# Projection stage of a decoder kernel: who copies the transposed tiles, and in which order VectorE and ScalarE take their steps

## What is computed

```
q = x Wq^T (32 heads of 128)   k = x Wk^T (8 heads)   v = x Wv^T (8 heads)
q, k = rmsnorm(q) * q_norm_w, rmsnorm(k) * k_norm_w      per head
q, k = rope(q), rope(k):  [t1 cos - t2 sin, t2 cos + t1 sin]
attention over 512 cached keys in pages and 32 new ones, then Wo
```

## Time and profile before

| what | value |
|---|---|
| median of three runs | 2634.18 us (2633.91 to 2634.66) |
| the profiled execution | 2633.39 us, its span 2631.6 us |
| busy over the span | PE 2530.8 us, VectorE 1653.0, ScalarE 1236.4, GpSimd 742.3 |
| projection stage | from the start to about 688 us |
| blocks of q and k | to about 608 us |

### The profile page before, as it was taken

One profiled execution on the slowest core, in us unless ns is written; L12 is line 12 of the kernel. 1 busy time (PEld: TensorE's weight loads), 2 busy tenths in 40 slices (PEclk: granted clock), 3 DMA queues, 4 the chain that ended last, 5 costly groups with the idle time before them and its releaser, 6 DMA issues. The chain is left out here.

```text
span 2631.6 us, 48525 instructions
## 1 busy us (share of the span) xinstructions
PE 2530.8 (96%) x15312; PEld 2178.8 (83%) x15312; DVE 1653.0 (63%) x3906; ACT 1236.4 (47%) x3285; POOL 742.3 (28%) x783
## 2 busy tenths in 40 slices
PE   5899999999999999999999999999998799999998
PEld 4677777778799999999999999999997577777776
DVE  8999999992366666666666666666666433333332
ACT  5555555552355555555555555555555222222221
POOL 5877777773021111211112111122111200000000
PEclk9999999999999999999999999999999899999999
DMA  3233233236598888888888888888885222322221
GB/s 139 81 97 94 82 112 90 86 96 211 164 340 272 265 267 265 270 274 267 265 263 270 272 272 265 266 267 266 283 258 192 80 90 90 96 84 88 88 87 44
DMA packets 369851, 484.13 MB, mean 184 GB/s; under 512 B 50320, under 2 KB 304528, under 8 KB 366480
## 3 DMA queue, kind: packets, MB, share of 16 engines
q1 hardware_dynamic: 332816, 347.67, 42.6%
q0 software_dynamic: 36864, 134.23, 14.3%
HBM read 393.70 MB, written 88.08 MB: 183 GB/s over the span
## 5 line engine op out<-in xcount | busy, mean ns | idle before, releaser
L821 ACT ACTIVATE probs<-probs,neg_max 128x544 f32<-128x544 f32 x512 | 383.5, 749 | 559.2 <-DVE neg_max L870 559.2
L893 PE MATMUL s_bank<-k_t,q_t 128*128 128x288 f32 (+1 forms) x2048 | 556.5, 394 | 4.6 <-POOL v_own L784 3.6
L910 PEld LDWEIGHTS o_bank<-p_t,v_c 128*128 128x128 f32 x4096 | 537.5, 192 | 26.3
L910 PE MATMUL o_bank<-p_t,v_c 128*128 128x128 f32 x4096 | 539.7, 275 | 0.0
L839 DVE COPY p_t<-pt_a 128x256 f32<-128x256 f32 x512 | 217.9, 426 | 417.4 <-PE pt_b L921 417.4
L893 PEld LDWEIGHTS s_bank<-k_t,q_t 128*128 128x128 f32 x2048 | 350.2, 191 | 60.0 <-POOL v_own L784 4.1
L441 POOL TENSOR_TENSOR q_t<-normed,v_c 128x256 f32<-128x256 f32 x320 | 337.8, 1076 | 147.8 <-ACT normed L490 147.8
L870 DVE CUSTOM_DVE_ANT_0 probs<-s_bank,mask 128x544 f32<-128x544 f32 x512 | 367.1, 717 | 3.9 <-PE s_bank L893 3.9
L656 PE MATMUL acc<-w_hi,x_hi 128*128 128x512 f32 x768 | 318.0, 414 | 14.7 <-DVE x_lo L541 14.7
L657 PE MATMUL acc<-w_lo,x_hi 128*128 128x512 f32 x768 | 304.4, 396 | 0.0
L658 PE MATMUL acc<-w_hi,x_lo 128*128 128x512 f32 x768 | 303.1, 395 | 0.0
(11 more groups left out here) (128 smaller groups left out, 3739.4 us busy)
## 6 DMA issues: line engine op xcount, KB each, us to landing
k_t<-in_k_pages SPq DMA_DIRECT2D x1024, 128.0 KB
q_spill<-wo_early SPq DMA_DIRECT2D x32, 1024.0 KB, 5.1
q_t<-q_spill SPq DMA_DIRECT2D x64, 512.0 KB
o_spill<-o_t SPq DMA_DIRECT2D x64, 512.0 KB, 8.8
raw<-o_spill SPq DMA_DIRECT2D x64, 512.0 KB, 3.5
k_t<-in_w_qkv SPq DMA_DIRECT2D x12, 1024.0 KB, 7.9
k_spill<-wo_early SPq DMA_DIRECT2D x8, 1024.0 KB, 5.1
v_spill<-wo_early SPq DMA_DIRECT2D x8, 1024.0 KB, 4.8
```

Source lines behind the costliest of these rows:

```text
L821: nc.scalar.activation(probs[:, j % 4], probs[:, j % 4], ACT.Exp, scale=-1.0, bias=neg_max[:, j % 2:j % 2 + 1], accum_out=row_sum[:, j % 2 ...
L893: last = pe.matmul(s_bank[:, columns].rearrange("p (s t) -> p s t", t=PSIZE), q_t[:, par, g], k_t[:, par, slots, g], start=True, stop=True)
L910: last = pe.matmul(o_bank, values, p_t[:, i, c], start=c == 0, stop=c == KC)
```

## The change

Three things change in the list of each engine for a q or k block:

- the copy of the transposed block n-4 moves from VectorE to ScalarE, ahead of the root;
- ScalarE drains block n-1 and then squares block n; before it was the other way round;
- VectorE multiplies block n-2 first, then takes the reciprocal of block n-1, adds block n-2, and sums block n's squares last.

TensorE, GpSimd and the queue of SyncE keep their lists.

```diff
 ScalarE, for each block
+                        if lag in ("q", "k"):
+                            m, t = n - 4, (j - 4) % NT
+                            act.wait_ge(flipped, m + 1)
+                            ...
+                            nc.scalar.activation(to.rearrange("p (b h s) -> p b h s", h=HS, s=S),
+                                                 flip[j % 2][:, :].rearrange("p (h b s) -> p b h s", h=HS, s=S),
+                                                 ACT.Copy).then_inc(staged_qk, 1)
...
                             nc.scalar.activation(rms[:, i], sumsq[:, i], ACT.Sqrt, bias=eps[:, 0:1], scale=1.0 / HD)
-                        if kind != "v":
-                            act.wait_ge(mm_done, n + 1)
-                            nc.scalar.activation(squares ... ACT.Square).then_inc(squared, 1)
                         if lag in ("q", "k"):
                             act.wait_ge(rstd_done, n)
...
                             last.then_inc(drained, 1)
+                        if kind != "v":
+                            act.wait_ge(mm_done, n + 1)
+                            nc.scalar.activation(squares ... ACT.Square).then_inc(squared, 1)
 VectorE, for each block
+                        rope = kind if j >= 2 else before
+                        m, i, t = n - 2, j % 2, (j - 2) % NT
+                        if rope in ("q", "k"):
+                            at_least(dve, roped_done, m)
+                            dve.wait_ge(drained, m + 1)
+                            nc.vector.tensor_tensor(part_s, normed[:, i], straight[rope] ..., ALU.mult)
                         if (kind if j >= 1 else before) in ("q", "k"):
                             dve.wait_ge(rooted, n)
+                            nc.vector.reciprocal(rstd[:, 1 - i], rms[:, 1 - i]).then_inc(rstd_done, 1)
+                        if rope in ("q", "k"):
+                            dve.wait_ge(straight_done, m + 1)
+                            dve.wait_ge(crossed_done, m + 1)
+                            at_least(dve, flipped, m - 1)
+                            nc.vector.tensor_tensor(roped[:, i], part_s, part_c[:, i], ALU.add)
-                        (the copy of flip to stage, with its waits on flipped and stored)
                         if kind != "v":
                             dve.wait_ge(squared, n + 1)
                             nc.vector.tensor_reduce(sumsq[:, j % 2], squares[:, j % 2], AX.X, ALU.add)
-                        (the product and the addition of block n-2, which stood here)
```

More of the change, by code:

```diff
@@ L476, in emit @@
                         n = p * PS + j
+                        lag = kind if j >= 4 else before
+                        if lag in ("q", "k"):
+                            m, t = n - 4, (j - 4) % NT
+                            act.wait_ge(flipped, m + 1)
+                            g, s2 = t // QUARTER, (p * 2 + (j - 4) // NT) * 2
+                            if t % QUARTER == 0:
+                                at_least(act, stored[g % 2], 16 * (s2 + g // 2))
+                            to = stage[:, g % 2, (t % QUARTER) * SLICE:(t % QUARTER + 1) * SLICE]
+                            nc.scalar.activation(to.rearrange("p (b h s) -> p b h s", h=HS, s=S),
+                                                 flip[j % 2][:, :].rearrange("p (h b s) -> p b h s", h=HS, s=S),
+                                                 ACT.Copy).then_inc(staged_qk, 1)
                         lag, i = (kind if j >= 1 else before), (j - 1) % 2
@@ L481, in emit @@
                                 .then_inc(rooted, 1)
-                        if kind != "v":
-                            act.wait_ge(mm_done, n + 1)
-                            nc.scalar.activation(squares[:, j % 2], acc[j % MM_BANKS][:, :].rearrange(
-                                "p (h d) -> p h d", d=HD), ACT.Square).then_inc(squared, 1)
                         if lag in ("q", "k"):
@@ L493, in emit @@
                             last.then_inc(drained, 1)
+                        if kind != "v":
+                            act.wait_ge(mm_done, n + 1)
+                            nc.scalar.activation(squares[:, j % 2], acc[j % MM_BANKS][:, :].rearrange(
+                                "p (h d) -> p h d", d=HD), ACT.Square).then_inc(squared, 1)
                         if kind == "v":
@@ L587, in emit @@
                         n = p * PS + j
+                        rope = kind if j >= 2 else before
[3 more added lines that the diff above has]
+                            dve.wait_ge(drained, m + 1)
+                            nc.vector.tensor_tensor(part_s[:, :, :], normed[:, i],
+                                                    straight[rope][:, t].unsqueeze(1).broadcast_to([P, HS, HD]),
+                                                    ALU.mult).then_inc(straight_done, 1)
                         if (kind if j >= 1 else before) in ("q", "k"):
-                            i = (j - 1) % 2
                             dve.wait_ge(rooted, n)
[L592 to L604, removed]
+                            nc.vector.reciprocal(rstd[:, 1 - i], rms[:, 1 - i]).then_inc(rstd_done, 1)
[3 more added lines that the diff above has]
+                            at_least(dve, flipped, m - 1)
+                            nc.vector.tensor_tensor(roped[:, i], part_s[:, :, :], part_c[:, i], ALU.add)\
+                                .then_inc(roped_done, 1)
                         if kind != "v":
@@ L612, in emit @@
                             page_rows()
[L614 to L626, removed]
                         if before is None and j in LATE:
```

## The result

The changed kernel takes 2605.26 us (median of four runs, 2604.74 to 2606.1), the kernel before on the same chip 2634.05: a ratio of 0.9893, with a 95% interval of 0.9876 to 0.991. A repetition gave 0.9904 (0.9889 to 0.9919), 2606.13 against 2631.88 us. The forecast was 2604.7.

What follows compares the result with a forecast made beforehand. VectorE and GpSimd excluding one another was taken to bound the projection stage, not VectorE's load. 26.5 us from 146 blocks plus 3 from the first 14 gave 29.5 off 2634.2: about 2604.7 us, range 2584 to 2622.

Steps and rivals of the forecast that it cites:

- The split's price in the kernel before: Projection stage before: a weight split on GpSimd adds 0.92 us to a block that otherwise takes 3.30 us.
- The lock: VectorE's two-SBUF-input instructions and GpSimd's exclude one another; VectorE's product, due at 2.23 us, is held to 2.64, ends at 3.19.
- The ring, 3.31 us: Block without a split: drain, GpSimd's crossed products, VectorE's held product, reciprocal, next drain take 3.31 us, where it took 3.30.
- The split after, 0.15 us: Changed kernel: a weight split costs about 0.15 us instead of 0.92, since the product no longer meets the 1.28 us subtraction.
- The copy at nothing: Moving the copy to ScalarE, about 0.60 us each, relieves no contention and costs nothing up to about 0.8 us.
- D: Slower: the copy on ScalarE takes more than about 1.2 us and delays the blocks; at 1.6, 2668 us; chance 0.02.
- The sum: Projection stage: 2.9 us per 16 blocks, 26.5 over 146 blocks, plus 3 in the first 14: 29.5 us off.
- A: TensorE becomes the bound at 3.23 us a block, 51.7 for 16 blocks: 2586 us; chance 0.14.
- B: GpSimd's crossed products at 0.81 us make a block 3.47 us: 2630 us, within 0.2% of before; chance 0.09.
- C: Slower: VectorE's product waits for a whole split and both crossed products, 1.9 us a split: 2668 us; chance 0.06.

Runs made afterwards that it cites:

- shortened subtraction: GpSimd's weight-split subtraction cut from 512 to 64 columns in the kernel before: 16 blocks 52.9 us instead of 56.6; in the changed kernel 53.5 instead of 53.8.
- shortened crossed product: GpSimd's second crossed product cut to one of four heads in the changed kernel: 16 blocks in 51.5 us instead of 53.8.
- reciprocal first: Changed kernel with VectorE's reciprocal ahead of its product: 2583.74 us against the changed kernel's 2606.13; ratio 0.9819 to the kernel before.
- both orders alone: Changed kernel with the copy back on VectorE, between addition and sum: ratio 0.9954 to the kernel before, last v block at 663.4 us.

## Why the prediction was right

*The split's price in the kernel before.* Read as 0.92 us, 3.7 for 16 blocks. The shortened subtraction gave 3.7 back (56.6 to 52.9). Shown.

*The lock.* Forecast: the product ends 0.55 us behind GpSimd's second product, issued 2.23 behind the drain and held to 3.19. Measured: issued 2.27 behind the drain, ended at 3.21, 0.55 behind GpSimd. Shown by the shortened crossed product, which takes the hold away and the ring down to 3.08, forecast 3.03.

*The ring, 3.31 us.* Measured 3.33. The missing 0.02 are the pair's: it took 1.44, not 1.42. The hop to the drain is 0.03, as estimated.

*The split after, 0.15 us.* The three blocks with a split took 10.09, so 10.09 - 3 x 3.33 = 0.10 us; forecast 10.1. The mechanism is the one described, the product getting in between the two crossed products.

*The copy at nothing.* Shown twice: moved alone it brings 1.1 us, and in the new orders 0.6. On ScalarE it took 0.63 us, where 0.60 was estimated and 0.65 given as the bound, so D did not come either.

*The sum.* The whole was forecast at 29.5 us, and the stage gave 25.0. The term that was mis-sized is the gain of 2.9 us for 16 blocks, taken already from block 14 on. By the sum the lead at the transposes of blocks 15 and 31 (behind the matmuls of blocks 18 and 34) should be some 3.9 and 6.8 us, and it was 3.5 and 2.7. Behind them 22.7 us were forecast and 22.3 came. So the 3 us for the first 14 blocks and the steady part were about right, and the second slab, put at 2.9 us, gave nothing. That the median came out within 0.6 us of the forecast is partly luck: the sum is 4.5 us too large for the stage, and the last stage added 3.7 to the measured difference that no term had. The repeated pair's 25.7 is the better size.

*Why the second slab gains nothing* is not settled. Even the kernel with the reciprocal first takes 57.3 us from block 15 to block 31, against 51.7 in the later slabs, so there is another limit there. GpSimd makes the last of its key tables in this slab (L400, to 132 us); it was not tried with the tables taken out.

*The rivals.* A, TensorE's pace, did not come, but two variants that differ by one instruction's place reach it, and they are 22 us faster in the stage. A was priced at 51.7 for 16 blocks and 2586 us, and the one with the reciprocal first took 51.7 and 2583.7. B's longer crossed products and C's split in the ring are refuted by the 1.44 us pair and the 10.09 us.

The Trainium skill's rule ("SBUF — State Buffer", Who interferes with whom), that the lock is held for the whole instruction and the later one waits, agrees with each of these rows: GpSimd's cast takes 1.07 us behind VectorE's product where it took 0.61, and the copy out of PSUM is never held, 0.65 to 0.69 us on VectorE in all these runs.

## What to carry to other kernels

When two engines exclude one another, ask of each meeting which of the two instructions has slack behind it, and order the lists so that the one without slack never comes second; the total of work on the busiest engine said nothing here. Find the pace by splitting a stage into its kinds of block before costing a change: 3.53 us was 3.30 with 0.92 on every fourth, and only the latter could be won. Where several things change at once, make each alone: the piece that looked like the gain, 0.65 us a block off an engine that is 93% busy, was worth nothing, one of the reorderings cost 22 us once the copy had moved, and the best of the kernels, 2583.7 us, differs from the changed one by a single instruction's place. An event measures a stage only if the change leaves its place: at block 36 the squarings showed no lead (161.99 and 162.33 us), the transposes behind its matmuls 3.7 us (162.75 and 159.02).

## What the runs showed of the hardware

- VectorE and GpSimd hold one another up by whole instructions, in both directions: a 128x512 product of two SBUF inputs took 0.68 us free and 1.67 behind a 1.28 us subtraction, a 0.61 us cast took 1.07 behind VectorE.
- One chip ran the kernel before 4% slower (2741.8 us, and another 2698.6) with the projection stage unchanged: the kernel with the reciprocal first starts its last cast at 561.91 us on the slow chip and at 561.86 on the usual one. In attention, from 700 to 1900 us, its TensorE was busy 1130 of 1200 us there and 1200 on the usual one, and the DMA moved 248 instead of 270 GB/s. What slows attention there was not looked into. To compare variants of one stage, events inside it were far sharper than the whole time.
- ScalarE's squaring took a mean of 615 to 616 ns in the kernels in which it waits for nothing (the changed one, both orders alone, reciprocal first with the copy on VectorE) and 590 to 601 where it waits for the matmuls, behind the drain too (601 with the reciprocal first); what lengthens it was not looked into.
